# GpSimd's select as the causal mask in four more steps of a fused attention and feed-forward kernel

## The chip, the cores and the metric
The kernel runs on one core of one Trainium2 chip. The metric is the device time of one execution in microseconds (us); lower is better. Three executions of the kernel before took 2751.12, 2753.20 and 2755.61 us, median 2753.2.

## The reference
The input is x of 16 batches x 512 tokens x 256 features in fp32. One pre-norm layer is computed: `x = x + attention(layernorm(x))`, then `x = x + ffn(layernorm(x))`.

```
q: 32 heads of 64; k, v: 16 heads of 64, each shared by 2 query heads
scores = q k^T / 8 + slope[head] * (key_pos - query_pos)       # ALiBi
scores = where(query_pos >= key_pos, scores, -inf)             # causal
out    = softmax(scores) v;   x = x + out @ W_out
ffn(x) = gelu((x @ U1) @ V1 + b1) @ U2 @ V2 + b2               # rank 64, 1024 wide
```

## The kernel before
fp32 accuracy comes from fp16 halves: a value is kept as a high part and a low part (value minus high part), and a product is made of three matmuls. For the softmax weights this means three engines in a row. ScalarE (ACT) takes the exponential from PSUM into `p_f` (fp32, L858) and then copies it to the high part `p_hi` (L808). GpSimd (POOL) subtracts, `p_lo = p_f - p_hi` (L1264). TensorE then multiplies both with v; this is called the attend (`o_acc`).

The order of work is written out by hand. The kernel walks over batches (i = 0 to 15, and two more rounds that drain the pipeline), each of 16 steps s, one for each k/v head, each of 5 segments n. Every engine has its own list of instructions, made by the same loops, and runs it strictly in that order; semaphores hold it until its input is there. The softmax work of a k/v head is done 7 steps after its q and k projections (`ATT = 7`), so the scores in step 15 are those of head 8 of the batch and those in step 6 are of head 15 of the batch before.

In segment n of a step TensorE computes score block n. It is 512 columns wide and transposed (keys in the partitions, queries in the columns). Blocks 0 and 1 hold one piece each, blocks 2, 3 and 4 two pieces each. Each piece has its diagonal 128x128 square at its start, and there the mask is needed. There are two ways to make it:

- by TensorE: a product of a constant (0 and -1e30) with the identity is added to the square in PSUM (L591 and L592, "causal product"); a block with two pieces has two of them;
- by GpSimd: the product is left out, the exponential is taken unmasked, and GpSimd sets the forbidden weights in `p_f` to zero with one affine select over both squares (L1258). ScalarE's `p_hi` of this block then waits for the select (`masked`), not for its own exponential.

`POOL_MASKS` lists the (step, block) pairs that are done the second way: blocks 2, 3 and 4 of steps 0, 2, 4, 5, 8, 9, 10 and 11. `mask_count` (L84) turns a pair into the number of selects that must have finished.

Around it the order on each engine is as follows.

- TensorE, segment n: scores(n); in segment 1 of steps 13, 15, 1 and 3 the first matmuls of a pair of feed-forward chunks; the row maxima's products; projections; in segment 1 and 3 the attend of the step before (h = 0 and 1). The attend with h = 0 waits for all five `p_lo` of that step. scores(n) waits for exp(n-2).
- ScalarE, segment n: q's high part in one of the segments, then p_hi(n-1), then exp(n). In segment 1 of steps 13, 15, 1 and 3 two gelus follow, with a change of the activation table before them and one before the next exp. In segment 4 comes the high part of the attend's output (`o_hi_lo`), and in segment 0 of the next step p_hi(4).
- GpSimd, segment n: the select of block n, if it is in the list, then p_lo(n-1). In segment 0 it is p_lo(4) of the step before, then the low part of the attend's output (L1278). In segment 2 of steps 13, 15, 1 and 3 two low parts of the feed-forward's hidden values follow (`h_lo`, L1296). Steps 9 to 13 have small operations of the second layernorm besides.
- In steps 2, 6, 10 and 14 the row maxima of four heads are transposed after scores of block 2 (TensorE), copied by ScalarE behind exp(2), split by VectorE and sent by a DMA into the q operands. The scores of the next step wait for that DMA.

The batch's feed-forward part runs in steps 8 to 15 of the next batch and in steps 0 to 5 of the one after. Batch 0 has none in its step 15, the 15 others have it.

Of the kernel before, what the change touches and what calls it, by code (L numbers as in the profile page):

```python
# [34 lines left out]
KV = 16  # L35
# [6 lines left out]
SEG = 5  # L42
AUG = 10
AUG0, MAX0 = 64, 96
ATT = 7
# [31 lines left out]
DVE_PARTS = 4  # L77
W_AT = {(0, 0): 4, (1, 3): 5, (2, 3): 6, (3, 3): 7}
SMALL_AT, WO_AT = (4, 3), {(5, 3): 0, (6, 3): 1}
MASK_STEPS = (0, 2, 4, 5, 8, 9, 10, 11)  # L80
POOL_MASKS = [(s, n) for s in MASK_STEPS for n in range(2, SEG)]


def mask_count(i, s, n):  # L84

    return i.value() * len(POOL_MASKS) + POOL_MASKS.index((s, n)) + 1 - len([m for m in POOL_MASKS if m[0] < ATT])


ST1_AT = {(4 + t, 2): t for t in range(T)}
# [148 lines left out]
def in_stage(mode, s, lag):  # L238

    return s >= lag if mode == FIRST else s < lag if mode == LAST else mode == MID  # L240


def layer(nc, x, w_qkv, w_out, u1, v1, b1, u2, v2, b2, k_aug, q_aug, ident_d, ident_b_d, causal_d, out):
    B = x.shape[0]
    ctx = ExitStack()
    with ctx:
# [286 lines left out]
        def _(pe):  # L533
# [5 lines left out]
            def mm(out_ap, lhs, rhs, start, stop):  # L539
                return nc.tensor.matmul(out_ap, lhs, rhs, start=start, stop=stop, skip_group_check=True)  # L540
# [23 lines left out]
            def body(i, mode):  # L564
# [10 lines left out]
                def scores(s, n):  # L575
# [10 lines left out]
                    for h, kt, off, width in SCORE_BLOCKS[n]:  # L586
# [3 lines left out]

                        if (s, n) not in POOL_MASKS:  # L591
                            mm(o[:, 0:P], causal[:, S - P:S], ident_b[:, :], False, False)  # L592
# [213 lines left out]
        def _(act):  # L806
# [41 lines left out]
            def body(i, mode):  # L848
# [11 lines left out]
                def high_p(s, n):  # L860
                    a = i * KV + s - ATT
                    if (s % KV, n) in POOL_MASKS:
                        act.wait_ge(masked, mask_count(i, s, n))
                    else:
                        act.wait_ge(exp_done, at(SEG * a + n + 1))

                    if 2 * a + AV_BEFORE[n] > 0:
                        act.wait_ge(pe_av, at(2 * a + AV_BEFORE[n]))
                    copy(p_hi[:, p_place(s, n), :], p_f[:, n, :]).then_inc(hi_p, 1)
# [339 lines left out]
        def _(pool):  # L1209
# [42 lines left out]
            def body(i, mode):  # L1252
                def mask(s, n):

                    pool.wait_ge(exp_done, at(SEG * (i * KV + s - ATT) + n + 1))
                    step = DIAGONAL[n][1] // P
                    both = p_f[:, n, :].rearrange("p (b q) -> p b q", q=P)[:, 0:step + 1:step, :]
                    nc.gpsimd.affine_select(both, both, [[0, 2], [1, P]], ALU.is_ge, 0.0, base=0,  # L1258
                                            channel_multiplier=-1).then_inc(masked, 1)
# [7 lines left out]
                for s in steps(mode):  # L1267
                    for n in range(SEG):
                        if (s, n) in POOL_MASKS and in_stage(mode, s, ATT):
                            mask(s, n)  # L1270
# [88 lines left out]
```

## Time and profile before
One execution was profiled.

| | |
|---|---|
| median of 3 executions | 2753.2 us (2751.12 to 2755.61) |
| the profiled execution's own time | 2755.59 us |
| span in its trace | 2753.5 us |
| mean granted TensorE clock | 0.989 of 2.4 GHz |
| busy: TensorE, GpSimd, ScalarE, VectorE | 2638.1, 2170.1, 2160.9, 1999.5 us |
| causal products, selects | 1280, 384 |

The table's busy times are unions: overlapping instructions of one engine count once. In the rows further down, PE is TensorE's matmuls, ACT ScalarE, POOL GpSimd, DVE VectorE. All times count from the start of the span. An idle time in brackets is the time in which the engine did nothing before the row's first instruction, with the instruction that ended it. Successive instructions of one engine overlap by some 0.04 us on GpSimd and 0.1 us on ScalarE, and matmuls by more, so a start is read against the next start.

### The profile page before, as it was taken

To read this page: it belongs to the slowest core of one execution; us is meant where nothing else is said; L and a number is where in the kernel's file an instruction comes from. 1 tells how busy PE (TensorE), PEld (TensorE's weight loads), DVE (VectorE), ACT (ScalarE), POOL (GpSimd) and SP (SyncE) were. 2 spreads that over 40 slices of the span, in tenths; PEclk is the share of its full clock that TensorE was granted. 3 is DMA by queue.
4 is the path that set the end of the run, shared out by engine and by line. 5 is a ranking of instruction groups with operands and counts; after the bars stand their busy time and mean duration, and the time that the engine had idled before them with its cause. 6 is when DMAs were issued, how large, how long until landed. Compare 5 with 4: busy or idle time off the path is not lost.

```text
span 2753.5 us, 83206 instructions
## 1 busy us (share of the span) xinstructions
PE 2638.1 (96%) x30344; PEld 1793.8 (65%) x30344; DVE 1999.5 (73%) x6825; ACT 2160.9 (78%) x3888; POOL 2170.1 (79%) x2221
## 2 busy tenths in 40 slices
PE   5999999999999999999999999999999999999985
PEld 2666666666666666666666666667666666666663
DVE  5678777776777777777776777778677786776753
ACT  4877878878788887878878788887878878887882
POOL 4878778787877878788787887878788787887884
PEclk8999999999999999999999999999999999999997
DMA  6444444444445445444444444444444444544421
GB/s 181 99 97 96 93 97 93 97 94 92 98 89 105 92 90 102 93 96 97 95 95 91 98 91 99 95 93 95 93 103 91 91 101 90 100 93 95 97 49 31
DMA packets 489111, 260.74 MB, mean 95 GB/s; under 512 B 310064, under 2 KB 485168, under 8 KB 488704
## 3 DMA queue, kind: packets, MB, share of 16 engines
q1 hardware_dynamic: 488704, 255.44, 44.9%
q8 instruction: 241, 3.95, 0.6%
q14 instruction: 166, 1.36, 0.2%
HBM read 27.73 MB, written 8.39 MB: 13 GB/s over the span
## 4 chain that ended last, share of the span: by engine, by line
PE 71%; ACT 9%; issue 8%; POOL 7%; DMA 3%; DVE 2%; SPq 1%; ACTq 0%; POOLq 0%; DVEq 0%
PE proj L540 34%; PE scores L540 17%; PE o_acc L540 12%; PE max_scores L540 8%; POOL p_lo L1264 4%; ACT p_hi L808 2%; ACT p_f L858 2%; ACT L858 2%; ACT h_f L953 2%; POOL h_lo L1296 2%; DMA o_t<-o_hi_lo 1%; DMA q_operands<-neg_max_t_lo 1%; PE proj L702 1%; DVE xn_t_lo L979 0%; POOL o_hi_lo L1278 0%
## 5 line engine op out<-in xcount | busy, mean ns | idle before, releaser
L1264 POOL TENSOR_TENSOR p_lo<-p_f,p_hi 128x512 f16<-128x512 f32 x1280 | 1483.9, 1169 | 372.8 <-ACT p_hi L808 372.0
L1038 DVE CUSTOM_DVE_ANT_0 max_scores<-max_scores,causal 128x512 f32<-128x512 f32 (+3 forms) x2048 | 971.1, 506 | 399.3 <-PE max_scores L540 359.9
L808 ACT ACTIVATE p_hi<-p_f 128x512 f16<-128x512 f32 x1280 | 800.6, 625 | 93.4 <-POOL p_f L1258 84.1
L858 ACT ACTIVATE p_f<-scores 128x512 f32<-128x512 f32 x1280 | 752.8, 588 | 151.4 <-PE scores L540 124.3
L540 PE MATMUL scores<-q_operands,k_lo_hi 128*128 128x512 f16 (+3 forms) x2048 | 607.2, 300 | 23.7 <-ACT p_f L858 17.2
L540 PE MATMUL scores<-q_operands,k_hi_aug 128*128 128x512 f16 (+3 forms) x2048 | 564.9, 299 | 0.0
L540 PE MATMUL o_acc<-v_hi_one,p_lo 128*128 128x65 f16 x5120 | 518.1, 194 | 34.4 <-POOL p_lo L1264 33.6
L540 PE MATMUL o_acc<-v_hi_one,p_hi 128*128 128x65 f16 x5120 | 517.7, 194 | 0.0
L540 PE MATMUL o_acc<-v_lo,p_hi 128*128 128x64 f16 x5120 | 517.1, 193 | 0.0
L540 PEld LDWEIGHTS o_acc<-v_hi_one,p_lo 128*128 128x128 f16 x5120 | 470.9, 98 | 68.9 <-POOL p_lo L1264 48.2
L540 PE MATMUL max_scores<-k_hi_aug,q_operands 96*128 96x512 f16 (+3 forms) x2048 | 491.8, 302 | 12.0 <-DMA k_lo_hi<-k_pair_lo 8.5
L540 PEld LDWEIGHTS o_acc<-v_lo,p_hi 128*128 128x128 f16 x5120 | 468.5, 98 | 38.8
L540 PEld LDWEIGHTS o_acc<-v_hi_one,p_hi 128*128 128x128 f16 x5120 | 467.7, 97 | 0.0
L540 PE MATMUL proj<-wo_hi,o_t 128*128 128x256 f16 x2016 | 372.1, 273 | 3.2 <-DMA o_t<-o_hi_lo 3.0
L540 PE MATMUL proj<-xn_t_hi,wqkv_lo 128*128 128x512 f16 x768 | 295.2, 384 | 5.1 <-DVE k_pair_lo L979 3.2
L1278 POOL TENSOR_TENSOR o_hi_lo<-o_f,o_hi_lo 128x512 f16<-128x512 f32 x256 | 296.7, 1159 | 4.1 <-ACT o_hi_lo L808 4.1
L540 PE MATMUL proj<-xn_t_lo,wqkv_hi 128*128 128x512 f16 x768 | 294.0, 383 | 0.0
L540 PE MATMUL proj<-xn_t_hi,wqkv_hi 128*128 128x512 f16 x768 | 293.8, 383 | 0.0
L1038 DVE DVE_READ_ACCUMULATOR2_ANT row_max<- 128x1 f32 x2048 | 281.6, 138 | 1.3
L540 PEld LDWEIGHTS scores<-q_operands,k_lo_hi 128*128 128x128 f16 x2048 | 199.6, 97 | 123.8 <-ACT p_f L858 25.2
L540 PE MATMUL scores<-ident_bf,causal 128*128 128x128 bf16 x1280 | 280.1, 219 | 0.0
L540 PE MATMUL proj<-wo_lo,o_t 128*128 128x256 f16 x1008 | 274.5, 272 | 0.0
(133 smaller groups left out, 4392.5 us busy)
## 6 DMA issues: line engine op xcount, KB each, us to landing
q_operands<-q_pair_hi SPq DMA_DIRECT2D x512, 128.0 KB, 2.5
q_operands<-q_pair_lo SPq DMA_DIRECT2D x512, 64.0 KB, 2.1
k_hi_aug<-k_pair_hi SPq DMA_DIRECT2D x256, 64.0 KB, 2.0
k_lo_hi<-k_pair_hi SPq DMA_DIRECT2D x256, 64.0 KB, 2.0
k_lo_hi<-k_pair_lo SPq DMA_DIRECT2D x256, 64.0 KB, 2.0
x_rows<-in_L_attn_inputs SPq DMA_DIRECT2D x17, 512.0 KB, 4.3
x_acc<-in_L_attn_inputs SPq DMA_DIRECT2D x64, 128.0 KB, 2.4
out<-x_rows SPq DMA_DIRECT2D x16, 512.0 KB, 3.2
```

Of the source, the lines that this page charges most:

```text
L540: return nc.tensor.matmul(out_ap, lhs, rhs, start=start, stop=stop, skip_group_check=True)
L702: last = nc.tensor.transpose(bank[:, c * P:(c + 1) * P], x2n[:, c * P:(c + 1) * P], ident[:, :])
L808: return nc.scalar.activation(out_ap, in_ap, ACT.Copy, scale=scale)
L858: nc.scalar.activation(p_f[:, n, :], score_bank[(SEG * s + n) % 2][:, :], ACT.Exp).then_inc(exp_done, 1)
L953: nc.scalar.activation(h_f[:, c % 2, :], h_place(f, c)[:, :], ACT.Gelu_apprx_tanh, bias=b1c[:, c:c + 1], scale=1.0 / FFN_SCALE).then_inc(g ...
L1038: last = nc.vector.tensor_tensor_reduce(out=bank, in0=bank, in1=causal[:, (T - 1 - qt) * P:S], scale=1.0, scalar=-3e38, op0=ALU.add, op1=A ...
L1264: nc.gpsimd.tensor_tensor(p_lo[:, place, :], p_f[:, n, :], p_hi[:, place, :], ALU.subtract).then_inc(lo_p, 1)
L1278: nc.gpsimd.tensor_tensor(o_hl[:, slot, 1, :], o_f[:, slot, :, :].rearrange("p t c -> p (t c)"), o_hl[:, slot, 0, :], ALU.subtract).then_i ...
L1296: nc.gpsimd.tensor_tensor(h_lo[:, c % 2, :], h_f[:, c % 2, :], h_hi[:, c % 2, :], ALU.subtract).then_inc(lo_h, 1)
```

## The change
Steps 15 (blocks 2, 3 and 4), 6 and 14 (blocks 2 and 3) and 12 (block 2) get GpSimd's select in place of the causal products. `MASK_STEPS` becomes a table of blocks by step. `mask_count` is taught that block 4 of step 15 is read in step 0 of the next batch (there as step -1). Eight blocks a batch change, and 128 in all.

```diff
-MASK_STEPS = (0, 2, 4, 5, 8, 9, 10, 11)
-POOL_MASKS = [(s, n) for s in MASK_STEPS for n in range(2, SEG)]
+MASK_STEPS = {0: (2, 3, 4), 2: (2, 3, 4), 4: (2, 3, 4), 5: (2, 3, 4), 6: (2, 3), 8: (2, 3, 4), 9: (2, 3, 4),
+              10: (2, 3, 4), 11: (2, 3, 4), 12: (2,), 14: (2, 3), 15: (2, 3, 4)}
+POOL_MASKS = [(s, n) for s, blocks in MASK_STEPS.items() for n in blocks]
 
 def mask_count(i, s, n):
 
-    return i.value() * len(POOL_MASKS) + POOL_MASKS.index((s, n)) + 1 - len([m for m in POOL_MASKS if m[0] < ATT])
+    done = (i.value() if s >= 0 else i.value() - 1) * len(POOL_MASKS)
+    return done + POOL_MASKS.index((s % KV, n)) + 1 - len([m for m in POOL_MASKS if m[0] < ATT])
```

## Rows read from the trace of the kernel before

**Rows 1.** The page: busy us (share of the span) and instructions by engine
```profile
PE 2638.1 (96%) x30344; PEld 1793.8 (65%) x30344; DVE 1999.5 (73%) x6825; ACT 2160.9 (78%) x3888; POOL 2170.1 (79%) x2221
```
**Rows 2.** TensorE's waits, whole span: total us, times, longest us
```profile
PE o_acc L540 <- POOL p_lo L1264: 33.6, 39, 1.9
...
PE scores L540 <- DMA q_operands<-neg_max_t_lo: 6.2, 8, 1.2
```
**Rows 3.** Groups by form, whole span: count | busy us, mean ns | idle us before
```profile
L540 PE MATMUL scores<-ident_bf,causal 128*128 128x128 bf16 x1280 | 280.1, 219 | 0.0
...
L1258 POOL TENSOR_SCALAR_AFFINE_SELECT p_f<-p_f 128x256 f32<-128x256 f32 x384 | 157.1, 409 | 129.7 <-ACT p_f L858 118.0
```
**Rows 4.** TensorE in order of time (start us, us): block 2, step 15, step 0
```profile
1302.01 0.33 PE L540 MATMUL scores<-q_operands,k_lo_hi 128*128 128x384 f16 x1
...
1302.55 0.38 PE L540 MATMUL max_scores<-k_hi_aug,q_operands 96*128 96x512 f16 x1
...
1310.64 0.33 PE L540 MATMUL scores<-q_operands,k_lo_hi 128*128 128x384 f16 x1
...
1311.08 0.38 PE L540 MATMUL max_scores<-k_hi_aug,q_operands 96*128 96x256 f16 x2
```
**Rows 5.** GpSimd in order of time, step 15 from its segment 2 on
```profile
1302.28 1.40 POOL L1264 TENSOR_TENSOR p_lo<-p_f,p_hi 128x512 f16<-128x512 f32 x1 [2.43 <-ACT p_hi L808]
1303.64 2.27 POOL L1296 TENSOR_TENSOR h_lo<-h_f,h_hi 128x512 f16<-128x512 f32 x2
1305.88 2.26 POOL L1264 TENSOR_TENSOR p_lo<-p_f,p_hi 128x512 f16<-128x512 f32 x2
1308.51 1.16 POOL L1264 TENSOR_TENSOR p_lo<-p_f,p_hi 128x512 f16<-128x512 f32 x1 [0.37 <-ACT p_hi L808]
```
**Rows 6.** ScalarE in order of time, the same stretch
```profile
1302.22 1.28 ACT L858 ACT_TABLE_LOAD   x1
1303.51 0.60 ACT L858 ACTIVATE p_f<-scores 128x512 f32<-128x512 f32 x1
...
1306.17 0.58 ACT L858 ACTIVATE p_f<-scores 128x512 f32<-128x512 f32 x1
1307.28 0.63 ACT L808 ACTIVATE o_hi_lo<-o_f 128x512 f16<-128x512 f32 x1 [0.54 <-DVE o_f L1081]
```
**Rows 7.** TensorE in order of time, step 0: scores(1), maxima, first attend
```profile
1307.40 0.38 PE L540 MATMUL scores<-q_operands,k_lo_hi 128*128 128x512 f16 x1
...
1308.03 0.39 PE L540 MATMUL max_scores<-k_hi_aug,q_operands 96*128 96x384 f16 x2
...
1309.72 0.20 PE L540 MATMUL o_acc<-v_hi_one,p_lo 128*128 128x65 f16 x1 [1.30 <-POOL p_lo L1264]
```
**Rows 8.** GpSimd in order of time, step 0: a select and the next p_lo
```profile
1314.47 0.41 POOL L1258 TENSOR_SCALAR_AFFINE_SELECT p_f<-p_f 128x256 f32<-128x256 f32 x1 [0.99 <-ACT p_f L858]
1314.85 1.15 POOL L1264 TENSOR_TENSOR p_lo<-p_f,p_hi 128x512 f16<-128x512 f32 x1
```
**Rows 9.** ScalarE in order of time, around that select
```profile
1313.81 0.59 ACT L858 ACTIVATE p_f<-scores 128x512 f32<-128x512 f32 x1
1314.91 0.63 ACT L808 ACTIVATE p_hi<-p_f 128x512 f16<-128x512 f32 x1 [0.51 <-POOL p_f L1258]
```
**Rows 10.** VectorE in order of time, step 15: the two casts
```profile
1301.91 0.76 DVE L1155 CAST h_hi<-h_f 128x512 f16<-128x512 f32 x2
```
**Rows 11.** GpSimd in order of time: last p_lo of steps 6 and 14
```profile
1381.48 1.16 POOL L1264 TENSOR_TENSOR p_lo<-p_f,p_hi 128x512 f16<-128x512 f32 x1 [1.55 <-ACT p_hi L808]
...
1295.67 1.16 POOL L1264 TENSOR_TENSOR p_lo<-p_f,p_hi 128x512 f16<-128x512 f32 x1 [1.25 <-ACT p_hi L808]
```
**Rows 12.** Windows: length, busy us of PE, PEld, DVE, ACT, POOL (x), clock, DMA
```profile
2689.83:2693.24 3.41, 1.88 (x39) 1.47 (x39) 0.45 (x2) 2.35 (x6) 3.41 (x4) 1.00 0.22 77
...
2696.66:2700.07 3.41, 1.09 (x30) 0.97 (x30) 0.70 (x3) 0.50 (x1) 2.72 (x3) 1.00 0.00 0
2700.07:2703.48 3.41, 3.13 (x38) 2.67 (x39) 0.83 (x3) 0.53 (x1) 0.00 (x0) 0.50 0.40 77
```

## The prediction
> **What bounds the kernel now.** I read the page first: TensorE is busy 2638.1 of 2753.5 us, and the reader is to see that no other engine is above 79% [rows 1]. The next question is what ends TensorE's idle stretches, and that is the view of waits of TensorE: 33.6 us of its idle time stand before an attend, ended by GpSimd's p_lo (39 times); 6.2 us stand before scores, ended by the DMA that lays out the row maxima (8 times) [rows 2]. So a TensorE instruction taken out is worth its own time wherever TensorE doesn't wait, and one us more in GpSimd's chain is worth a full us where an attend already waits for p_lo. The third view is the order of time on each engine around one boundary. I take batch 7's step 15 and the step 0 after it (1295.3 to 1318.3 us); the middle batches repeat it to 0.1 us. There TensorE is at work without a marked gap until the first attend of step 0, which waits 1.30 us for p_lo of step 15 [rows 7]. A wait of about that length stands at that place in each of the 15 batches that run a feed-forward part in step 15.
>
> **What it removes.** A masked step gives up, for each block, two products with the causal constant. Such a product takes 219 ns from start to end [rows 3], but matmuls overlap, so its price is the spacing. A block with both products takes 1302.01 to 1302.55 = 0.54 us until the next matmul, one of the same shape without them 1310.64 to 1311.08 = 0.44 [rows 4]: 0.10 for two; I use 0.055 each, since rounding allows 0.050 to 0.060. Eight blocks a batch are 16 products, 256 in all, 14.1 us if all of it counts.
> The Trainium skill, "TensorE: Matmul & The Clock Gate", section "Back-to-back issue gap", gives about 81 ns as sustained spacing for 128 columns. By it the 256 products would be worth 20.7 us; the trace's 0.05 disagrees, and the trace is used.
>
> **What it adds.** A select of 128x256 on GpSimd, mean 409 ns [rows 3]. The instruction behind it starts 0.38 us after the select's start (1314.47 to 1314.85) [rows 8], so each moves GpSimd's queue by 0.38. The select starts 0.07 after exp's end (1313.81 + 0.59 = 1314.40) [rows 8, 9], and ACT's p_hi of that block starts 0.03 after the select's end (1314.88 to 1314.91) [rows 8, 9]. There are two new waits. GpSimd waits at the select of block n for exp(n), and behind it in the queue stands p_lo(n-1), then in step 15 the two h_lo. ACT waits at p_hi(n) for the select, and behind it stands exp(n+1).
>
> **Steps 6, 12, 14.** Each ends with p_lo of its last block after GpSimd sat idle: 1.55 us in step 6, 1.25 in step 14 [rows 11]; step 12 has the same pattern with one select to hold. GpSimd waits there for ACT's p_hi of a block, which in turn stands behind work that ends later. Two selects move GpSimd's queue by 0.76 us, one by 0.38. Taking both queues through in order (each select behind its exp, each p_hi behind its select), ACT comes 0.4 to 0.9 us later in the middle of the step and is back before the last p_hi, so the last p_lo starts as before and the cover holds. Were it gone, every 0.1 us of delay at one of these attends would cost 16 x 0.1 = 1.6 us. Gain: 5 blocks x 2 x 16 x 0.055 = 8.8 us. The row maxima's DMA limits it: its chain starts with exp of block 2, only one block's 0.11 earlier, while TensorE arrives 0.22 earlier. It ended TensorE's idle time 8 times in the run [rows 2]; with all of them put here, 8 x 0.11 = 0.9 is lost. Net -7.9 us, with ends of -8.8 and 0.
>
> **Step 15.** Here segment 1 has two gelus with a table load on either side, and exp of block 2 comes only after the second load: 1302.22 + 1.28, then exp 1303.51 to 1304.11 [rows 6]. GpSimd now uses that time: p_lo(1) runs at 1302.28, the two h_lo from 1303.64, p_lo(2) and p_lo(3) from 1305.88 to 1308.14, p_lo(4) from 1308.51 to 1309.67 [rows 5]. TensorE's attend follows at 1309.72 [rows 7]. With the selects in GpSimd's program order:
> - select(2) waits for exp(2): 1304.11 + 0.07 = 1304.18. p_lo(1) stands behind it and starts at 1304.56 in place of 1302.28: +2.28.
> - p_lo(1) now takes 1.16, not 1.40: the 1.40 stood beside the two casts of VectorE (1301.91 to 1302.67) [rows 5, 10]. h_lo twice is 2.24 more (1303.64 to 1305.88): select(3) starts at 1304.56 + 1.12 + 2.24 = 1307.92 and ends at 1308.33.
> - ACT's p_hi(3) waits for it: 1308.36 to 1308.99, and exp(4), which stands behind, runs from 1308.89 to 1309.47 in place of 1306.17 [rows 6].
> - p_lo(2) 1308.30 to 1309.46; select(4) waits for exp(4) + 0.07: 1309.54 to 1309.95; p_lo(3) from 1309.92, p_lo(4) from 1311.04 to 1312.20.
> - ACT's o_hi copy, which waited 0.54 for VectorE [rows 6], is off the path: it runs at 1309.4, p_hi(4) at 1310.0, before p_lo(4) needs it.
> The attend starts at 1312.25 in place of 1309.72: +2.5 us. Step 15's own saved products bring nothing. Those of blocks 2 and 3 end in the wait for exp(2) before scores of block 4, those of block 4 end in this longer wait, which is set by GpSimd. Nothing gives the 2.5 us back: after the attend GpSimd, ACT and TensorE stand as before, all 2.5 later. Times 15 batches: 37.5 us. Bounds: 0.8 a batch (three selects of 0.38 less the 0.37 that GpSimd waits before p_lo(4) [rows 5], if the wait for exp(2) cost nothing) and 2.9 (if the 0.37 came back, because p_hi(4) is late again). Batch 0 has no feed-forward part in step 15; I leave it at zero (-0.3 to +1.0).
> The Trainium skill, "GPSIMD Engine Reference", section "1. Specifications", says that GpSimd shares its SBUF interfaces with VectorE and contends with its 2-port modes or instructions with two SBUF inputs. The 1.40 beside the casts agrees. If the 0.24 were not saved, because another such instruction met p_lo, the sum would be 15 x 0.24 = 3.6 us higher.
>
> **TensorE's clock.** The new stall is in two parts. scores of block 1 in step 0 waits for exp(4), until 1309.5 in place of 1307.40; with its max product it takes 1.02 (1307.40 to 1308.42) [rows 7]; then comes the wait until 1312.25. So over 4.8 us (1307.45 to 1312.25) TensorE works for only 1.0. In the tail of this trace TensorE worked 1.09 of 3.41 us at 2.4 GHz and the next 3.41 ran at 0.50 (1.2 GHz); after 1.88 of 3.41 it stayed at 1.00 [rows 12]. So the clock can fall at this place. A fall like that one costs at most half of 3.41 = 1.7 us. Between 0 and 15 of the batches can have it, 0 to 25.6 us. I take 4, 6.8 us: only a stretch as empty as that one can be named, and the place also has busier surroundings.
>
> **Sum.** Against the profiled execution's own 2755.59 us (span 2753.5 and 2.1 around it): 2755.6 + 37.5 - 7.9 + 6.8 = 2792.0. That execution stands 2.4 above the median 2753.2 of the runs, so the forecast of the median is 2789.6, rounded 2790, 1.3% slower.
>
> **Rivals.**
> - *The clock falls in every batch.* 2753.2 + 37.5 - 7.9 + 25.6 = 2808.4. For it speaks that the stall is alike each time; against it that a fall shifts all that follows against the clock. Chance 0.08.
> - *Only the selects' own time counts.* If p_lo(1) weren't held by exp(2), the boundary would move by 1.14 less the 0.37 us that GpSimd waits before p_lo(4) [rows 5] = 0.77, times 15 = 11.6, and with the -7.9 the median is 2756.9. It needs p_lo(1) ahead of select(2) in GpSimd's queue, and the code has it behind. Chance 0.08, half of it within 0.2%.
> - *Faster.* If step 15's chain had room for the selects, all 256 products count: 2753.2 - 14.1 = 2739.1. It decides by whether p_lo(4) of step 15 ends by 1308.4, when TensorE is ready for the attend. It now ends at 1309.67, already 1.3 too late [rows 5, 7], so masks there would have to make GpSimd's chain shorter. Chance 0.05.
> - *A further stall.* If the attends after steps 6 and 14 come to wait 0.5 us each, 16 us are added: 2806. Against it stand the 1.25 and 1.55 idle us [rows 11]. Chance 0.09.
>
> **How the numbers follow.** The forecast case (2.0 to 3.0 us a batch at this boundary, up to 10 falls) holds 0.70; its own range is 2776 to 2805. Range for 8 in 10: 2776 to 2808. About 0.2% (5.5 us) is what a measurement of this kernel can tell from no change. Faster 0.05, same 0.04, slower 0.91.
>
> **What would show it.** At the boundary of steps 15 and 0, TensorE's waits for GpSimd's p_lo and ACT's exp should add to about 3.8 us in place of 1.3, in 15 batches. GpSimd's first select of step 15 should wait for exp over 4 us after p_lo(0) ended, with p_lo(1) behind it, 2.3 later than before against the step's start. 1024 causal products and 512 selects should stand in the groups. Clock intervals of 0.50 may stand in the middle of the span, each behind step 0's first scores. Steps 7, 13 and step 15's start should show no new wait for p_lo. The prediction is wrong if step 0 takes less than 13 us, or if the loss sits in steps 6, 12 or 14.

## The result, and the profile after

The changed kernel takes 2819.66 us (median of 4, 2816.43 to 2823.08) against 2754.01 (median of 4 beside it). The ratio is 1.0241, 95% interval 1.0227 to 1.0255: 66 us slower. The forecast was 2790 with a range of 2776 to 2808; the sign was right. The forecast loss of 36 us is a little over half of the measured one, and the whole range lies below the measured time.

The reading begins with the busy times, the waits of TensorE and the groups, as in [rows 1 to 3]. Line numbers are 2 higher than before.

The busy row of the changed kernel's page:
```profile
PE 2663.2 (94%) x30088; PEld 1798.3 (64%) x30088; DVE 2001.3 (71%) x6825; ACT 2163.7 (77%) x3888; POOL 2216.8 (79%) x2349
```
The waits of TensorE (total us, times, longest us):
```profile
PE scores L542 <- ACT p_f L860: 46.8, 60, 2.2
PE o_acc L542 <- POOL p_lo L1266: 41.3, 39, 2.9
...
PE scores L542 <- DMA q_operands<-neg_max_t_lo: 5.6, 9, 1.3
```
The wait for exp in the kernel before:
```profile
PE scores L540 <- ACT p_f L858: 17.2, 45, 2.0
```
The groups by form:
```profile
L542 PE MATMUL scores<-ident_bf,causal 128*128 128x128 bf16 x1024 | 224.0, 219 | 0.0
...
L1260 POOL TENSOR_SCALAR_AFFINE_SELECT p_f<-p_f 128x256 f32<-128x256 f32 x512 | 209.8, 410 | 247.8 <-ACT p_f L860 230.6
```
There are 256 fewer products, as forecast, yet TensorE's busy time rose by 25.1 us (2638.1 to 2663.2). That can't come from a wait; only slower matmuls do that. It is the first hint at the clock. The waits for p_lo grew by 7.7 us, and TensorE's scores now wait 46.8 us for ScalarE's exp; before it was 17.2.

The same boundary, step 15 of batch 7 and step 0 behind it, stands 28.34 us later than in [rows 5 to 7] (step 0 starts at 1335.04 in place of 1306.70). GpSimd in order of time (an "x2" at the end of a row is two instructions taken together):
```profile
1332.52 0.41 POOL L1260 TENSOR_SCALAR_AFFINE_SELECT p_f<-p_f 128x256 f32<-128x256 f32 x1 [4.33 <-ACT p_f L860]
1332.90 1.17 POOL L1266 TENSOR_TENSOR p_lo<-p_f,p_hi 128x512 f16<-128x512 f32 x1
1334.02 2.27 POOL L1298 TENSOR_TENSOR h_lo<-h_f,h_hi 128x512 f16<-128x512 f32 x2
1336.24 0.41 POOL L1260 TENSOR_SCALAR_AFFINE_SELECT p_f<-p_f 128x256 f32<-128x256 f32 x1
1336.61 1.16 POOL L1266 TENSOR_TENSOR p_lo<-p_f,p_hi 128x512 f16<-128x512 f32 x1
1337.87 0.41 POOL L1260 TENSOR_SCALAR_AFFINE_SELECT p_f<-p_f 128x256 f32<-128x256 f32 x1
1338.24 2.27 POOL L1266 TENSOR_TENSOR p_lo<-p_f,p_hi 128x512 f16<-128x512 f32 x2
```
ScalarE in order of time:
```profile
1331.85 0.60 ACT L860 ACTIVATE p_f<-scores 128x512 f32<-128x512 f32 x1
...
1336.68 0.63 ACT L810 ACTIVATE p_hi<-p_f 128x512 f16<-128x512 f32 x1 [2.60 <-POOL p_f L1260]
1337.22 0.58 ACT L860 ACTIVATE p_f<-scores 128x512 f32<-128x512 f32 x1
```
TensorE in order of time, the two waits and then one of the projection's matmuls:
```profile
1337.85 0.39 PE L542 MATMUL scores<-q_operands,k_lo_hi 128*128 128x512 f16 x1 [1.94 <-ACT p_f L860]
1340.57 0.24 PE L542 MATMUL o_acc<-v_hi_one,p_lo 128*128 128x65 f16 x1 [1.83 <-POOL p_lo L1266]
...
1343.46 0.63 PE L542 MATMUL proj<-xn_t_hi,wqkv_lo 128*128 128x512 f16 x1
1343.89 0.63 PE L542 MATMUL proj<-xn_t_lo,wqkv_hi 128*128 128x512 f16 x1
```
The reader is to see the forecast's chain row by row. The select of block 2 waits for exp(2) with GpSimd idle for 4.33 us and p_lo(1) behind it. The two h_lo come before the select of block 3. ScalarE waits 2.60 us for that select, and exp(4) is late behind it. TensorE waits 1.94 + 1.83 = 3.77 us where 1.30 stood. The last two rows are what the forecast had too small: matmuls of 512 columns start 0.43 us apart. In the kernel before the same two start 0.22 apart:
```profile
1311.30 0.38 PE L540 MATMUL proj<-xn_t_hi,wqkv_lo 128*128 128x512 f16 x1
1311.52 0.38 PE L540 MATMUL proj<-xn_t_lo,wqkv_hi 128*128 128x512 f16 x1
```

The windows view around it (from and to, length, busy us of PE, PEld, DVE, ACT, POOL with the number of instructions, granted clock, DMA share, GB/s; PEld is TensorE's weight loads):
```profile
1335.75:1339.17 3.42, 1.04 (x6) 0.37 (x5) 3.04 (x10) 2.49 (x5) 3.32 (x5) 1.00 0.15 32
1339.17:1342.58 3.41, 2.02 (x32) 1.85 (x33) 0.78 (x5) 2.00 (x4) 3.41 (x4) 0.50 0.00 0
1342.58:1346.00 3.42, 3.42 (x12) 1.46 (x11) 1.33 (x6) 0.60 (x1) 1.68 (x3) 0.50 0.40 77
1346.00:1349.40 3.40, 3.40 (x49) 2.52 (x48) 2.34 (x6) 2.55 (x5) 1.51 (x2) 1.00 0.35 74
```
TensorE had worked 1.04 of 3.42 us, much as in the tail before [rows 12]. It then stood at half clock (1.2 GHz) for 6.83 us. That is twice the length of the row on which the forecast had rested, and most of the second wait (1338.73 to 1340.57) lies in its first part. Step 0 of the batches 7, 8 and 9 in the same view, with the clock as the third value from the end:
```profile
1164.33:1181.02 16.69, 12.92 (x117) 7.99 (x115) 9.52 (x32) 9.06 (x16) 12.62 (x16) 0.80 0.28 58
1335.04:1351.71 16.67, 12.89 (x117) 7.93 (x114) 9.52 (x32) 9.06 (x16) 12.61 (x16) 0.80 0.27 57
1504.83:1520.24 15.41, 11.64 (x116) 7.66 (x114) 9.52 (x32) 9.06 (x16) 12.62 (x16) 0.89 0.30 62
```
Step 0 of batch 8 in the kernel before:
```profile
1306.70:1318.29 11.59, 10.29 (x117) 6.67 (x115) 9.25 (x32) 7.99 (x15) 9.85 (x12) 1.00 0.40 84
```
In all 15 steps 0 behind a step 15 with a feed-forward part the clock fell: 12 rows show 0.80 or less, 3 show 0.89. A mean of 0.80 over 16.7 us is 6.7 us at half clock, 0.89 over 15.4 is 3.4. In the kernel before all 15 have 1.00. These 15 steps took 243.60 us in place of 171.43, that is 72.2 more. Step 15 itself took 0.2 us less over the whole run although six products a batch are gone from it, as forecast. The steps 6, 12 and 14 took 4.7, 1.8 and 3.1 us less over the whole run, and step 7 of batch 0 took 1.3 less; steps 2, 4 and 8 took 2.3 more, and the span's start and tail 1.9.

### The profile page after: what moved, and what is told of

Same layout as the page of the kernel before. It is cut to its first block, busy times and chain, and to the rows that moved or that the text cites. A ratio compares the mean times of both kernels' runs of the same rounds, so it can differ in the third digit from the quotient of the medians.

```text
span 2818.7 us, 82822 instructions
## 1 busy us (share of the span) xinstructions
PE 2663.2 (94%) x30088; PEld 1798.3 (64%) x30088; DVE 2001.3 (71%) x6825; ACT 2163.7 (77%) x3888; POOL 2216.8 (79%) x2349
## 4 chain that ended last, share of the span: by engine, by line
PE 69%; POOL 10%; ACT 8%; issue 7%; DMA 3%; DVE 1%; SPq 1%; ACTq 0%; POOLq 0%; DVEq 0%
PE proj L542 33%; PE scores L542 16%; PE o_acc L542 12%; PE max_scores L542 7%; POOL p_lo L1266 6%; POOL h_lo L1298 3%; ACT p_f L860 2%; ACT p_hi L810 2%; ACT L860 2%; ACT h_f L955 2%; DMA o_t<-o_hi_lo 1%; DMA q_operands<-neg_max_t_lo 1%; POOL p_f L1260 1%; PE proj L704 1%; POOL o_hi_lo L1280 0%
## 5 line engine op out<-in xcount | busy, mean ns | idle before, releaser
L542 PE MATMUL scores<-q_operands,k_lo_hi 128*128 128x512 f16 (+3 forms) x2048 | 611.0, 302 | 52.7 <-ACT p_f L860 46.8
L542 PE MATMUL o_acc<-v_hi_one,p_lo 128*128 128x65 f16 x5120 | 529.4, 196 | 42.1 <-POOL p_lo L1266 41.3
L542 PE MATMUL o_acc<-v_hi_one,p_hi 128*128 128x65 f16 x5120 | 529.2, 195 | 0.0
L542 PE MATMUL o_acc<-v_lo,p_hi 128*128 128x64 f16 x5120 | 528.5, 194 | 0.0
L542 PEld LDWEIGHTS o_acc<-v_hi_one,p_lo 128*128 128x128 f16 x5120 | 477.4, 99 | 77.1 <-POOL p_lo L1266 56.3
L542 PEld LDWEIGHTS o_acc<-v_lo,p_hi 128*128 128x128 f16 x5120 | 475.1, 100 | 39.1 <-issue 0.3
L542 PEld LDWEIGHTS o_acc<-v_hi_one,p_hi 128*128 128x128 f16 x5120 | 474.5, 98 | 0.0
L1260 POOL TENSOR_SCALAR_AFFINE_SELECT p_f<-p_f 128x256 f32<-128x256 f32 x512 | 209.8, 410 | 247.8 <-ACT p_f L860 230.6
L542 PEld LDWEIGHTS scores<-q_operands,k_hi_aug 128*128 128x128 f16 x2048 | 201.5, 98 | 118.0 <-issue 5.3
```

## The experiments

Each was compared with the kernel before on the same chip; ratios are with their 95% intervals. Theory A: step 15's selects make all of the loss, by a longer wait at the boundary and by the fall of the clock behind it.

**Without step 15's selects.**
```diff
-              10: (2, 3, 4), 11: (2, 3, 4), 12: (2,), 14: (2, 3), 15: (2, 3, 4)}
+              10: (2, 3, 4), 11: (2, 3, 4), 12: (2,), 14: (2, 3)}
```


> The changed kernel with step 15 back to the causal products; steps 6, 12 and 14 keep their selects. Theory A (all of the loss is made at the boundary of steps 15 and 0 by step 15's selects: a longer wait of TensorE, and a fall of its clock behind it): the changed steps give 0.22, 0.11 and 0.22 us a batch, so the time is 2754.0 - 8 = 2746 us, with the clock at 0.989 and step 0 at 11.59 us as before. Rival B (part of the loss lies in the other steps or in later DMA waits): over 2754.


Measured: 2742.8 us, ratio 0.9953 (0.9938 to 0.9967). The other three steps are a gain. Step 0 is back at 11.59 us with the clock at 1.00; here it is in batch 8:
```profile
1298.86:1310.45 11.59, 10.29 (x117) 6.67 (x115) 9.26 (x32) 7.99 (x15) 9.85 (x12) 1.00 0.39 82
```
Step by step against the kernel before, step 6 took 8.2 us less (3.5 of it are products, the rest fewer waits for the maxima's DMA), step 14 4.3 less, step 8 2.2 less, and step 12 3.5 more, because an output projection waited for its DMA in 9 batches. The sum over the steps is -10.9, of which steps 6, 12 and 14 have -9.0. Another 3.8 us of this execution's 14.7 lie at the span's start and tail, which the change doesn't touch: TensorE's first scores stand between 66.3 and 69.9 us in the traces of this record, whatever the change.

**Step 15's selects alone.** The entries of 6, 12 and 14 are left out.


> The kernel before with the selects of step 15 alone. Theory A: the changed kernel's 2819.7 plus the 8 us that the other three steps gave: 2827 us, clock 0.97, step 0 at 15.4 to 16.9 us. Rival B: well under 2820, because the other steps carry a share.


Measured: 2822.1 us, ratio 1.0242 (1.0226 to 1.0257). The loss is whole with step 15 alone, its steps 0 taking 72.0 us more than before. That is 5 us less than expected. Step by step against the changed kernel, steps 6, 12 and 14 took 9.8 us more, as they should, but step 8 took 2.6 less and the span's start and tail 7.4 less. Why step 8's waits and the start differ is not shown.

**The two waits filled.** While it would wait, TensorE multiplies weights into a free bank, and nobody reads the result; what it waits for is left as it is.
```diff
+FILL = (8, 7)
+    def fill(count):
+        if i.value() >= 2:
+            b = PROJ["q", 0]
+            pe.wait_ge(proj_free[b][0], at(proj_free[b][1]))
+            for _ in range(count):
+                mm(proj_bank[b][:, :], wqkv[0][:, 0, 0:P], wqkv[0][:, 0, 0:512], True, True)
     ...
+    if (s, n) == (0, 1):
+        fill(FILL[0])               # in scores, ahead of the wait for exp
     ...
+    if (s, h) == (0, 0):
+        fill(FILL[1])               # in attend, ahead of the wait for p_lo
```


> The changed kernel, and TensorE gets matmuls of 512 columns whose result nobody reads: 8 of them (1.7 us) ahead of the wait for exp(4) in step 0 (1.94 us long) and 7 (1.5 us) ahead of the wait for p_lo (1.83 us), both inside the waits, so that nothing is late by them. The stall stays as it is, only TensorE's emptiness goes. Theory A, with 35 us of the loss due to the clock (the 15 steps 0 took 72 us more than before, and the waits account for 37): 2820 - 35 = 2785 us, clock back to 0.99, no interval of 0.50 in the middle of the span. Rival B (the clock's fall costs nothing, since TensorE waits for others then anyway, and the 35 us have another cause): 2820.


Measured: 2784.4 us, ratio 1.0106 (1.0089 to 1.0123). Step 0 of batches 7 and 8, windows view:
```profile
1149.33:1163.42 14.09, 13.55 (x131) 8.05 (x129) 9.52 (x32) 9.06 (x16) 12.62 (x16) 1.00 0.35 67
1317.02:1331.12 14.10, 13.56 (x132) 8.06 (x130) 9.52 (x32) 9.05 (x16) 12.62 (x16) 1.00 0.32 67
```
Fifteen useless matmuls a batch make the kernel 35 us faster. Step 0 usually takes 14.09, which is 11.59 plus 2.50, against 2.47 of longer wait (3.77 - 1.30), and all 15 rows have a clock of 1.00. The 15 steps 0 take 209.1 us, 37.7 more than before and 34.5 less than in the changed kernel. This splits the loss at the boundary into some 37 us of wait and 35 us of clock. The rival that the fall costs nothing is out.

**Selects of blocks 3 and 4 only.** `15: (3, 4)`


> The changed kernel, but step 15 has the selects of blocks 3 and 4 only; p_lo(1) no longer stands behind a wait for exp(2). Working through the queues: p_lo(4) ends at 1310.1 in place of 1309.7, so the attend of step 0 is 0.46 us later, 15 x 0.46 = 7 us. Theory A (the wait for exp(2) ahead of p_lo(1) is the main term): 2754 - 8 + 7 = 2753 us, no clock fall. Rival C (the selects cost through ACT's p_hi(3) and exp(4), whichever block is first): 1.5 us or more a batch, 2770 and up.


Measured: 2768.2 us, ratio 1.0046 (1.0031 to 1.0061). Two neighbouring steps 0, batches 8 and 9:
```profile
1311.40:1325.08 13.68, 11.91 (x116) 7.44 (x114) 9.41 (x32) 8.65 (x16) 10.57 (x13) 0.88 0.32 67
1479.31:1491.36 12.05, 10.28 (x116) 6.58 (x114) 9.41 (x32) 8.65 (x16) 10.59 (x13) 1.00 0.38 80
```
TensorE's wait in these two batches:
```profile
1314.88 0.20 PE L542 MATMUL o_acc<-v_hi_one,p_lo 128*128 128x65 f16 x1 [1.76 <-POOL p_lo L1266]
...
1482.80 0.20 PE L542 MATMUL o_acc<-v_hi_one,p_lo 128*128 128x65 f16 x1 [1.77 <-POOL p_lo L1266]
```
The queues were worked out rightly: 12.06 is 0.47 over 11.59 (expected 0.46), and TensorE's wait is 1.77 in place of 1.30. But "no clock fall" was wrong: 8 of the 15 rows have 0.88 and 1.65 us more. 15 x 0.47 + 8 x 1.65 = 20.2, just what these steps took over before. The total lies near rival C's 2770, but not by rival C's mechanism: its 1.5 us a batch of longer wait are not there. In these two batches the wait and the work beside it are the same, and only one has a fall. So something that changes from batch to batch decides too; the moment at which the wait comes is the nearest candidate, and it was not varied.

**The same, its wait filled.** FILL = (0, 7) in the kernel of blocks 3 and 4.


> The selects of blocks 3 and 4 in step 15 (with those of 6, 12 and 14), and 7 matmuls of 512 columns (result unused) in TensorE's wait of 1.77 us before the attend of step 0. If the 25 us by which blocks 3 and 4 stand over the kernel without step 15's selects are 15 x 0.47 = 7 us of longer wait and the rest the clock: 2742.8 + 7 = 2750 us, no interval of 0.50 in the middle of the span. If the rest has another cause: 2768.


Measured: 2754.4 us, ratio 0.9998 (0.9989 to 1.0007). All 15 rows have 1.00, and 14 us of the 25 are gone. Of the 11.8 us between this profiled execution and that of the kernel without step 15's selects, steps 0 have 7.8, where 7 were worked out, and the span's start 3.2. Step 6 took 5.3 us more, where the maxima's DMA is waited for again, and step 12 took 4.9 less.

**Select of block 2 only.** `15: (2,)`


> The changed kernel, but step 15 has the select of block 2 alone. Theory A by the queues: p_lo(1) starts 2.28 us later behind the select's wait for exp(2), the two h_lo, p_lo(2), (3) and (4) follow without a gap, and the attend of step 0 comes 1.65 us later; exp(4) is not held, so TensorE has one unbroken wait of 1.30 + 1.65 = 2.95 us. Without a fall of the clock 2742.8 (no selects in step 15) + 15 x 1.65 = 2767.6 us; with one fall of 3.41 us (1.65 us lost, as measured with blocks 3 and 4) at each boundary 2792. Rival C (the selects cost through ACT's p_hi(3) and exp(4), so block 2's, which delays neither, costs little): 2743 to 2750.


Measured: 2792.4 us, ratio 1.0139 (1.0118 to 1.0159). TensorE's attend waits 2.93 us in each of the 15 batches, here in batch 8:
```profile
1327.92 0.24 PE L542 MATMUL o_acc<-v_hi_one,p_lo 128*128 128x65 f16 x1 [2.94 <-POOL p_lo L1266]
```
Of the rows 13 have a clock under 1.00, nine of them for 3.41 us and four for 6.83. That the median meets the expected 2792 is in part luck, as that figure had 15 falls of 3.41. The four executions of this kernel took 2786.3 to 2798.3 us at a mean clock of 0.986 to 0.980 (the profiled one was the longest), so the falls differ from execution to execution. So block 2's select, which holds up p_lo(1) and hardly anything of ScalarE's, costs more than blocks 3 and 4 together (1.63 us of longer wait against 0.47). The rival by which the loss runs through p_hi(3) and exp(4) alone is out.

**Only the second wait filled.** FILL = (0, 7) in the changed kernel.


> The changed kernel with only the second of the two waits filled (7 matmuls of 512 columns, result unused). TensorE is then empty for 1.94 us in one piece. If any wait near 2 us can bring the clock down (9 of 15 boundaries had a fall beside a single wait of 1.77 us with the selects of blocks 3 and 4), 9 to 15 falls of 1.65 us come on top of the filled kernel's 2784: 2799 to 2809 us. If it takes both waits together: 2784.


Measured: 2785.2 us, ratio 1.0111 (1.0096 to 1.0126). TensorE is empty for 2.02 us in one piece, here in a batch with a fall (7) and in one without (8):
```profile
1155.90 0.38 PE L543 MATMUL scores<-q_operands,k_lo_hi 128*128 128x512 f16 x1 [2.04 <-ACT p_f L873]
...
1324.53 0.38 PE L543 MATMUL scores<-q_operands,k_lo_hi 128*128 128x512 f16 x1 [2.03 <-ACT p_f L873]
```
```profile
1153.00:1168.30 15.30, 13.27 (x124) 8.20 (x121) 9.51 (x32) 9.05 (x16) 12.62 (x16) 0.89 0.30 61
...
1321.63:1335.97 14.34, 11.97 (x123) 7.26 (x121) 9.52 (x32) 9.05 (x16) 12.87 (x16) 1.00 0.32 66
```
The first figure of the expectation failed: only 3 of 15 rows show a fall. The time fits the second figure, 2784, but it doesn't take both waits together either, since three rows fell. With blocks 3 and 4 a shorter wait of 1.77 had 8 falls (the expectation says 9; the rows show 8). So the length of one wait doesn't tell. Two things differ and neither was varied alone: the work behind the wait (scores of 512 columns and the filling here, the attend's many products of 65 columns there) and the moment at which it comes. The work can't be the whole of it, since with blocks 3 and 4 the same work had a fall in 8 batches and none in 7.

**p_lo ahead of the select.** In step 15 GpSimd runs p_lo(n-1) before the select of block n.
```diff
-                        if (s, n) in POOL_MASKS and in_stage(mode, s, ATT):
+                        if s != 15 and (s, n) in POOL_MASKS and in_stage(mode, s, ATT):
                             mask(s, n)
                         if n > 0 and in_stage(mode, s, ATT):
                             low_p(s, n - 1)
+                        if s == 15 and (s, n) in POOL_MASKS and in_stage(mode, s, ATT):
+                            mask(s, n)
```


> The changed kernel, but in step 15 GpSimd runs p_lo(n-1) ahead of the select of block n; the two h_lo stay where they are. This is the order that the prediction's rival 'only the selects' own time counts' asked for (2757 us). Theory A by the queues says that it saves almost nothing: p_lo(1) runs at 1302.3 and select(2) at 1304.2, but the two h_lo end at 1306.8, p_lo(2) at 1308.0, select(3) at 1308.3; ACT's p_hi(3) and exp(4) behind it end at 1309.5 as before, p_lo(4) at about 1312.4. So the same two waits, and 2815 to 2823 us. A figure near 2757 would say that the select's wait for exp(2) ahead of p_lo(1) was the whole of it.


Measured: 2826.3 us, ratio 1.0260 (1.0244 to 1.0276). GpSimd in order of time:
```profile
1332.33 1.40 POOL L1266 TENSOR_TENSOR p_lo<-p_f,p_hi 128x512 f16<-128x512 f32 x1 [2.42 <-ACT p_hi L810]
1334.23 0.41 POOL L1260 TENSOR_SCALAR_AFFINE_SELECT p_f<-p_f 128x256 f32<-128x256 f32 x1 [0.50 <-ACT p_f L860]
1334.61 2.27 POOL L1300 TENSOR_TENSOR h_lo<-h_f,h_hi 128x512 f16<-128x512 f32 x2
1336.84 1.15 POOL L1266 TENSOR_TENSOR p_lo<-p_f,p_hi 128x512 f16<-128x512 f32 x1
1337.95 0.41 POOL L1260 TENSOR_SCALAR_AFFINE_SELECT p_f<-p_f 128x256 f32<-128x256 f32 x1
1339.10 1.16 POOL L1266 TENSOR_TENSOR p_lo<-p_f,p_hi 128x512 f16<-128x512 f32 x1 [0.74 <-ACT p_hi L810]
```
p_lo(1) is back in its old place and took its 1.40 beside the casts again. But this order also puts p_lo(2) ahead of the select of block 3, which therefore starts 1.20 us behind the start of step 0 in this kernel (1336.75) as in the changed one (1335.04), and now GpSimd also waits 0.74 before p_lo(3). TensorE's first wait is 1.94 as in the changed kernel, the second 2.13 in place of 1.83. The prediction's rival "only the selects' own time counts" needed p_lo(1) ahead of the select of block 2. With it the time is not 2757 but 2826, somewhat over the expected 2815 to 2823: what p_lo(1) gave back, p_lo(2) took again. An order with p_lo(1) alone ahead of its select was not tried.

**A shorter chain.** No selects in step 15; the second h_lo of step 15 runs behind step 0's `o_hi_lo` on GpSimd; ScalarE copies o_hi of step 15 behind p_hi(4).
```diff
+    low_h = [2 * pair] if (s, n) == (15, 2) and not at_end(f) else [2 * pair, 2 * pair + 1]
+if (s, n) == (0, 0) and ffn_in(i, s) and not at_end(ffn_batch(i, s)):
+    f, low_h = ffn_batch(i, s), [3]
     ...
-    if n == O_SEG and in_stage(mode, s, ATT + 1):
+    if s != KV - 1 and n == O_SEG and in_stage(mode, s, ATT + 1):
+        high_o(i, s)
     ...
     high_p(s - 1, SEG - 1)
+    if s == 0:
+        high_o(i - 1, KV - 1)
```


> The kernel without step 15's selects, and two instructions moved out of the way of p_lo(4) of step 15: the second h_lo of that step runs on GpSimd behind the o_hi_lo of step 0, and ACT copies o_hi of step 15 behind p_hi(4), not ahead of it. Theory A (the wait of 1.30 us before the attend is GpSimd's and ACT's order in step 15, with two h_lo of 1.12 and the copy's wait of 0.54 on it): p_lo(4) ends at 1308.6 in place of 1309.7, 1.1 us a batch: 2742.8 - 16 = 2727 us. Rival D (another wait stands right behind, of VectorE or a DMA): 2738 or more.


Measured: 2729.9 us, ratio to the kernel before 0.9914 (0.9898 to 0.9931). Step 0 of batches 7 and 8:
```profile
1130.87:1141.68 10.81, 10.46 (x117) 6.67 (x115) 9.17 (x32) 8.01 (x15) 10.28 (x12) 1.00 0.44 93
1295.38:1306.19 10.81, 10.46 (x116) 6.67 (x114) 9.16 (x32) 8.01 (x15) 10.27 (x12) 1.00 0.43 88
```
With the variant that follows it is the fastest. Step 0 takes 10.81 in place of 11.59, and the attend's wait is 0.28. The gain is 0.78 a batch, not 1.1: 12 us of the expected 16. The two moves were made together, so the share of each is not known.

**All of step 12.** `12: (2, 3, 4)` in the kernel with the shorter chain.


> The kernel with the shorter chain (no selects in step 15, the second h_lo and the o_hi copy moved), with all three blocks of step 12 on GpSimd in place of block 2 alone. Theory A: GpSimd is idle for 1 us in step 12 and the attend of step 13 has 1.46 us to spare, so two more blocks give 4 products x 0.055 x 16 = 3.5 us: 2729.9 - 3.5 = 2726. Rival: GpSimd's operations of the second layernorm in step 12 have no room for it, and the time is 2730 or more.


Measured: 2732.5 us, ratio 0.9917 (0.9900 to 0.9934), no gain. Step 12 took 5.6 us less than in the kernel it was made from, steps 8 and 14 took 5.0 and 3.0 more. The rival's reason, no room on GpSimd in step 12, is out, since step 12 itself gained. The products went; waits in other steps took their place (in step 8 the output projection's marked waits for its DMA went from none to 4.6 us).

## Why the prediction was wrong

- **What bounds the kernel: right.** TensorE, with the attend of step 0 as the place where GpSimd's chain ends. Step 15's selects alone make the loss.
- **The price of a product: right.** 0.11 for a block's two: step 12's usual time went from 8.93 to 8.82, step 6's from 8.24 to 8.02, step 14's from 9.45 to 9.23.
- **Steps 6, 12 and 14: right.** Their cover held, nothing new waits for p_lo there. The forecast -7.9 stands against -9.6 in these steps of the changed kernel and -9.0 in the kernel without step 15's selects (whose -13 as a whole holds step 8, the start and the tail besides). That it is so near is in part luck: the products' share was right, but the 0.9 us that were to be lost to the maxima's DMA were not, as TensorE's waits for it fell from 6.2 to 5.6 us, and step 12's waits for another DMA moved by some us.
- **Step 15's chain: right, to 0.1 us.** Its term was 2.5 us a batch and 37.5 in all. The trace shows 3.77 - 1.30 = 2.47, and with the clock held up by filling step 0 takes 2.50 more. The two parts of the stall, the 1.0 us of work between them, and the order of the queue behind each select came out as worked out.
- **TensorE's clock: the step that failed.** The term was "I take 4, 6.8 us", from "a fall like that one costs at most half of 3.41 = 1.7 us". Two things were off. The number: 15 of 15 fell. The stretch that the term itself had described, 1.0 us of work in 4.8, is as empty as the row it cited, 1.09 of 3.41 [rows 12], and nothing in the profile spoke for it being spared in 11 batches; four was a hedge, not a reading. (The shorter stalls of later runs were spared in some batches; this one fell in all 15 in three kernels: the changed one, the one with step 15's selects alone, and the one with p_lo ahead of the select.) The size: 12 of the 15 falls last 6.83 us and not 3.41. The rest of the stall lies inside the first 3.41 us at half clock, in which TensorE was busy for 2.02, and the next 3.41 stood at half as well. The measured price is 35 us for 15 falls, 2.3 us each, where 4 falls of 1.7 us, 6.8 in all, stood. Even the rival "the clock falls in every batch" at 2808.4 was too cheap, by the size alone. With the measured term the same sum gives 2755.6 + 37.5 - 7.9 + 35 - 2.4 = 2817.8, against 2819.7 measured.
- **The range: too low for the same reason.** Its upper end had been the clock's bound at 1.7 us a fall.

What is not settled: what decides on a fall, the work beside a wait or the moment at which it comes (1.77 us of wait had 8 of 15, 2.02 us with other neighbours 3 of 15, 2.93 had 13, 1.30 none), and what moves the waits for the maxima's and the output's DMAs from step to step by some us.

## What to carry to other kernels

Before an instruction is given to an engine that is idle on average, read what it will wait for and what stands behind it in that engine's queue: here one select of 0.41 us, waiting behind a table load with p_lo(1) behind it, made the attend wait 1.6 us longer. When a stall on TensorE grows, look at how much work stands in and around it, not at the stall alone: the clock's share here was as large as the wait's, and a cheap trial is to fill the wait with matmuls nobody needs and see what comes back. Count the falls over all batches and executions, since the same wait can have one in one batch and none in the next. Where an order is changed to free one instruction, read what the new order holds up: p_lo(1) came free and p_lo(2) stood in the way of the next select. The gains came from masks in steps whose chains had room, and from taking work off the end of the chain that had none.

## What the runs showed of the hardware

- TensorE at half clock behind waits in the middle of a busy kernel, lasting 3.41 or 6.83 us. With the selects of blocks 3 and 4 a fall of 3.41 us cost step 0 some 1.65 us (13.68 to 13.74 in place of 12.06). In the changed kernel one of 3.41 us cost 1.3 to 1.6 and one of 6.83 us 2.1 to 2.8 (against the filled kernel's step 0 of the same batch).
- The same wait with and without a fall: with blocks 3 and 4 TensorE waited about 1.77 us (1.76 to 1.83) in 15 batches, and 8 had a fall.
- Useless work that gains time: 15 matmuls of 512 columns (3.2 us at full clock) put into two waits of 3.77 us gave 2.3 us a batch.
- p_lo(1) of step 15 took 1.40 us beside VectorE's two casts, in the kernel before and again where it was put ahead of the select, and 1.17 us in the changed kernel, where it runs later. The Trainium skill's "GPSIMD Engine Reference", section "1. Specifications", says that GpSimd shares its SBUF interfaces with VectorE, with contention for some kinds of VectorE instruction. The 1.40 agrees with the sharing; that the casts are of such a kind, no trace here shows.
